# A windowed-attention block on one core: the key-value products moved in front of the convolution

## What is computed

```python
x = x + conv_bn(x, dw0_w, dw0_s, dw0_b, groups=C)       # depthwise 3x3
x = x + ffn(x, f0...)                                   # 1x1, relu, 1x1
x = x + windowed_attn(x, ...)                           # 7x7 windows, 4 heads of 16 channels
x = x + conv_bn(x, dw1_w, dw1_s, dw1_b, groups=C)
x = x + ffn(x, f1...)

# attention, in each window:
q, k, v = xw @ wq.T, xw @ wk.T + pos, xw @ wv.T
q, k = focus((relu(q) + 1e-6) / sc), focus((relu(k) + 1e-6) / sc)
#   focus(t) = t**3 / norm(t**3) * norm(t)
z   = 1 / (q @ k.sum(over tokens) + 1e-6)
y   = (q @ (k.T @ v)) * z + dwc(v)                      # dwc: depthwise 5x5 in the window
out = y @ proj_w.T + proj_b
```

## Time and profile before

| | |
|---|---|
| time, median of 3 runs | 210.66 us (209.52 to 211.52) |
| the profiled execution | 209.91 us |
| its span in the profile | 208.1 us, 4705 instructions |
| TensorE busy (matmul) | 184.5 us, 89% |
| VectorE busy | 127.4 us, 61% |
| ScalarE busy | 94.3 us, 45% |
| GpSimd busy | 34.6 us, 17% |
| mean granted TensorE clock | 0.984 of full speed |

### The profile page before, as it was taken

How to read it: one execution, slowest core, us unless ns; L and a number is a source line. 1 busy time by engine, 2 the same in 40 slices (tenths; PEclk the granted TensorE clock), 3 DMA queues, 4 the chain that set the end, 5 groups by cost and what they waited for, 6 DMA issues and landing times.

```text
span 208.1 us, 4705 instructions
## 1 busy us (share of the span) xinstructions
PE 184.5 (89%) x1938; PEld 98.4 (47%) x1938; DVE 127.4 (61%) x235; ACT 94.3 (45%) x152; POOL 34.6 (17%) x78
## 2 busy tenths in 40 slices
PE   7699963997997997999899979979979999899883
PEld 6224621352753753884464546528447844522210
DVE  3748496295599599419948975975994183122111
ACT  2462813238159159423832652581395315322431
POOL 1000350007007107000430160070052000000000
PEclk9999998599999999999999999999999999999999
DMA  6999917624000000000430161171044007666912
GB/s 141 216 250 214 204 38 156 173 73 72 3 0 5 0 3 0 0 6 0 142 72 2 57 159 54 45 165 54 0 120 144 3 20 183 161 171 163 255 56 95
DMA packets 15092, 19.12 MB, mean 92 GB/s; under 512 B 2160, under 2 KB 10608, under 8 KB 15072
## 3 DMA queue, kind: packets, MB, share of 16 engines
q1 hardware_dynamic: 13744, 17.63, 35.6%
q10 hardware_dynamic: 1328, 1.20, 2.3%
HBM read 14.50 MB, written 4.33 MB: 90 GB/s over the span
## 4 chain that ended last, share of the span: by engine, by line
PE 74%; ACT 9%; DVE 6%; issue 4%; DMA 4%; SPq 0%; POOL 0%; DVEq 0%; ACTq 0%; POOLq 0%
PE ps L471 15%; PE ps L495 9%; PE ps L606 8%; ACT kv L382 6%; PE ps L558 6%; PE ps L512 4%; PE ps L538 4%; PE ps L660 4%; PE ps L489 4%; PE ps L577 4%; PE ps L623 4%; PE ps L562 3%; DMA xr<-x_out 2%; PE ps L666 2%; PE ps L516 2%
## 5 line engine op out<-in xcount | busy, mean ns | idle before, releaser
L471 PE MATMUL ps<-xr,dwst 96*32 96x480 f32 (+1 forms) x384 | 43.3, 584 | 3.5 <-DVE x L751 1.8
L320 POOL TENSOR_SCALAR vmt<-vbot,cst 128x128 f32<-128x128 f32 x48 | 17.3, 385 | 122.4 <-PE ps L562 99.5
L495 PE MATMUL ps<-hid,w2t 128*64 128x512 f32 x64 | 23.3, 645 | 10.2 <-ACT hid L344 10.2
L344 ACT ACTIVATE hid<-ps,fst 128x512 f32<-128x512 f32 x32 | 20.2, 690 | 12.9 <-PE ps L489 12.9
L471 PEld LDWEIGHTS ps<-xr,dwst 96*32 96x32 f32 x384 | 11.2, 111 | 28.1 <-issue 25.3
L336 ACT ACTIVATE x<-ps,fst 128x512 f32<-128x512 f32 x16 | 10.9, 684 | 24.8 <-PE ps L471 24.8
L489 PE MATMUL ps<-x,w1t 64*128 64x512 f32 x64 | 18.1, 640 | 4.3 <-ACT x L336 3.3
L359 ACT ACTIVATE sq<-tqk 128x1280 f32<-128x1280 f32 x8 | 10.2, 1271 | 24.1 <-DVE tqk L779 23.4
L382 ACT ACTIVATE kv<-ps,cst 128x288 f32<-128x288 f32 x32 | 19.2, 765 | 3.0 <-PE ps L562 2.8
L606 PEld LDWEIGHTS ps<-qt,kv 64*64 64x64 f32 x576 | 17.4, 135 | 4.9 <-issue 4.8
L771 DVE TENSOR_TENSOR kraw<-ps,pose 128x640 f32<-128x640 f32 x8 | 6.6, 824 | 21.1 <-PE ps L516 21.1
(11 more groups left out here) (105 smaller groups left out, 256.0 us busy)
## 6 DMA issues: line engine op xcount, KB each, us to landing
xr<-x_out SPq DMA_DIRECT2D x16, 264.0 KB, 4.6
xr<-in_x SPq DMA_DIRECT2D x16, 240.0 KB, 6.3
x_out<-x SPq DMA_DIRECT2D x8, 272.0 KB, 2.5
xr<-x_out SPq DMA_DIRECT2D x8, 272.0 KB, 3.3
xr<-in_x SPq DMA_DIRECT2D x8, 256.0 KB, 5.2
out<-y SPq DMA_DIRECT2D x8, 256.0 KB, 2.3
tband<-in_matrix ACTq DMA_DIRECT2D x1, 784.0 KB, 5.1
wts<-in_weights SPq DMA_DIRECT2D x1, 416.0 KB, 8.4
```

What stands on the lines that cost most here:

```text
L320: last = eng.tensor_scalar(vmt[:, w, :, :], vbot[:, g, :, :], cc("win_bot")[:, w:w + 1], 0.0, ALU.mult, ALU.add)
L344: eng.activation(hid[:, m % 2, a, :], bank(P_H + a), ACT.Relu, bias=ff(f"f{s}b1")).then_inc(h_ready, 1)
L471: last = eng.matmul(dst[:, :, max(-dx, 0):HW - max(dx, 0)], dwst[:, s, tile % 2, dx + 1, :], taps_of(m, tile, dx), start=(dx == 0), stop=( ...
L495: last = eng.matmul(dw_bank(m)[64 * a:64 * a + 64], w2t[:, s, :], hid[:, m % 2, a, :], start=True, stop=True)
```

## The change

In the loop TensorE computes `key_value(g2)` directly behind `key_sum(g2)`, in front of the convolution instead of behind `project_v(g1)`. ScalarE's `take_kv(g2)` moves with it, in front of `widened`, and `take_v(g1)` goes behind `sixth(g1)`. In front of the loop the order of the first three groups is another one on TensorE, ScalarE and VectorE. No instruction is added or taken away, no wait is changed, and GpSimd's and SyncE's programs stay as they are.

```diff
@@ ScalarE @@
             squares(0)
             widened(2)
+            sixth(0)
+            hidden(2)
             take_v(0)
-            hidden(2)
-            sixth(0)
             ratio(0)
             widened(3)
...
                 squares(g1)
+                take_kv(g2)
                 widened(n + AHEAD)
+                sixth(g1)
                 take_v(g1)
-                sixth(g1)
-                take_kv(g2)
                 hidden(n + AHEAD)
@@ TensorE @@
             conv(2)
+            project_qk(1)
+            ffn1(2)
             project_v(0)
-            ffn1(2)
-            project_qk(1)
             ffn2(2)
...
                 key_sum(g2)
+                key_value(g2)
                 conv(n + AHEAD)
                 if 0 <= c:
                     project(c)
                 project_v(g1)
-                key_value(g2)
                 ffn1(n + AHEAD)
@@ VectorE @@
             cubes(0)
+            norm2(0)
             k_raw(1)
             q_t(1)
             k_t(1)
             residual(2)
-            norm2(0)
+            norm6(0)
             eng.wait_ge(pads_ps, 1)
             eng.tensor_tensor(projc[:, :], bank(7)[:, 447:448], ff("projb"), ALU.add).then_inc(projc_read, 1)
             eng.tensor_copy(kf[96:128, 0:8, :], bank(7)[96:128, 448:512].unsqueeze(1).broadcast_to([32, 8, C]))
             eng.tensor_copy(kf[0:32, 8:10, :], bank(7)[0:32, 448:512].unsqueeze(1).broadcast_to([32, 2, C])).then_inc(pads_taken, 1)
-            norm6(0)
```

## The result

| | before | after |
|---|---|---|
| time, median | 210.75 us (209.52 to 211.52, 4 runs) | 198.69 us (198.39 to 201.8, 4 runs) |
| ratio of the two, 95% interval | | 0.943 (0.937 to 0.949) |
| the profiled execution, its span | 209.91, 208.1 us | 198.42, 196.7 us |
| TensorE busy | 184.5 us, 89% | 182.4 us, 93% |
| mean granted TensorE clock | 0.984 | 1.000 |

The account below looks back on a forecast made before the run. TensorE's chain bound the kernel, with ScalarE's order making hid late and a slow start. 6.0 + 1.46 + 4.40 - 0.4 = 11.5 us took the profiled 209.91 to 198.4, median 198.8; range 196.5 to 203.0.

Parts of the forecast that it names:

- start and pass 2: From the program's start to pass 3: reordered first groups and pass 2 make pass 3 begin at 48.2, gaining 6.0 us.
- of it the clock: At the start: TensorE keeps full clock instead of falling to half, about 2.5 us of the 6.0 gained.
- passes 3 and 4: Main loop: hid starts earlier despite a new 0.5 us stall for q_t; 0.73 us each, 1.46 for two.
- passes 5 to 7: Main loop: hid no longer waits behind take_kv, so each pass takes 16.19 instead of 17.29 us, gaining 1.10.
- pass 8: Last loop pass: gains 1.10 us but loses 0.4 because the window convolution's bank comes free late.
- rival (2): At the start the clock falls all the same: 2.5 us less gain, 201.3 us, chance 0.12.
- Passes 5 to 8: Main loop: no stall for q_t, turn_q hidden before ffn2's second half; 1.10 us a pass, 4.40 for four.
- VectorE's round: VectorE's work per loop pass: 15.9 to 16.0 us against TensorE's 16.19, hidden by 0.2 to 0.3.
- the 200.0 us: Loop: q_final and k_focus meeting GpSimd's masks cost 0.27 us each, VectorE binds at 16.5; 1.2 us in all.
- The rival of the masks (7): Slower kernel: GpSimd's masks, their slack cut from 10.8 to 3.9 us, delay key_value; some 213 us, chance 0.02.
- The tail: After pass 8: keeps its order and only moves, with no gain or loss counted.
- The cover for the transfers: Loop: transfers stay covered, as attended moves 1.7 us later and the conv reading its result 2.1 later.

Follow-up runs that it names:

- the queries first: Changed kernel with q_scale and q_final moved in front of attended on VectorE in the loop; 199.5 us, ratio 0.949.
- a third of the masks: Changed kernel with only three of nine GpSimd masks made for groups 1 to 7; 200.57 us.
- the old copies: Changed kernel with ScalarE's loop order as before the change, TensorE and the start as changed; 234.86 us, ratio 1.129.
- fillers behind it: Kernel before with eight extra matmuls, results unread, between conv(3) and ffn1(3) on TensorE; 210.38 us.

## Right or wrong, step by step

The prediction was right, and nearly term by term (us gained; the measured ones are from the two profiled executions):

| step | predicted | measured |
|---|---|---|
| start and pass 2 | 6.0 | 6.2 |
| of it the clock | 2.5 | 2.54 |
| passes 3 and 4 | 1.46 | 1.31 |
| passes 5 to 7 | 3.30 | 3.11 |
| pass 8 | 1.10 - 0.4 = 0.7 | 0.68 |
| sum | 11.5 | 11.3 |

That the median (198.69) came within 0.1 us of 198.8 is in part luck: the terms are off by 0.2, 0.15 and 0.19 with different signs, and the tail's wait for a transfer was 0.5 us in both profiled executions, though it is 1.4 us or more in eleven of the twelve other runs.

**The start.** `residual(2)` was put at 27.2 and came at 27.09, `conv(3)` at 28.1 (27.98), `x1(3)` at 30.85 (30.72), `ffn2(3)`'s end at 35.1 (35.01), pass 3 at 48.2 (48.03). Its parts are now separate: 2.63 from the order up to `ffn1(3)` (17.48 to 14.85 behind the first projection), 2.54 from the clock, 1.04 from the loop's order in pass 2. The judgement that the clock would stay up held: TensorE's waits were 0.26, 0.80 and 0.77 us (forecast 0.7, 0.8 and 0.8), so rival (2) did not come. The old order of VectorE, with 2.46 us in front of `ffn1(3)`, brings the fall back.

**Passes 3 and 4.** `key_value` waits 0.5 for `q_t`, as worked out, and ScalarE is tight behind it: `sixth`, `vband` and `vbot` are in the chain there. The gain is 0.15 smaller because each pass takes 0.1 more than the 15.15 and 20.04 that the terms gave: `key_value` starts 3.43 into the pass, not 3.33. `hid` starts at 10.65, where the prediction wrote 10.57 and its own terms add up to 10.50 to 10.55. And the last link is not `hid` alone: `turn_q`, which needs the copied values, is ready last by the chain, a link that the prediction doesn't have there.

**Passes 5 to 8.** The wait for `hid` is gone and no wait for `q_t` came. One word was wrong: `turn_q` was called hidden. It is the last to be ready, is over at 12.80 of the pass, and the whole of `ffn2` still follows it, up to 14.04; by way of `hid`, as the run with the queries first shows, it is 14.05. So two chains bind the pass, which the prediction did not see. The 0.05 us between 16.19 and 16.24 are not this: `key_value` takes 2.17 us (103.05 to 105.22), where the terms had 2.12. In pass 8 the loss is where it was forecast, at the window convolution's bank: 0.38 us over 16.24 + 4.89, against 0.4, and 0.35 of it goes away with the queries first.

**VectorE's round** was given 0.2 to 0.3 us of slack, and it has 0.1 (wait of 0.26 with a third of the masks, less the 0.16 that `k_focus` is shorter there) to 0.2 (band masks twice). The meeting with the masks is real but costs 0.16 us, not 0.54, and so the 200.0 us did not come: `q_final` takes 0.76 and 0.28 us as before, and only the first 0.3 us of `k_focus` lie beside a mask in pass 6. The Trainium skill, page "GPSIMD Engine Reference", section "1. Specifications", has the two engines contend for the shared interfaces when VectorE reads two SBUF inputs; `k_focus` does, and the traces agree (in pass 6: 1.29 us without masks beside it, 1.45 as changed, 2.24 and 5.34 beside more of them).

**The rival of the masks (7)** was put aside for a sound reason, nothing in the kernel makes masks of 8 us, but its deciding point was incomplete. The wait of `key_value` that it names does come when the masks last 9.4 us (43.4 to 52.8), in passes 3 and 4; the slack there is 3.1 us (masks end at 48.4, `key_value` starts at 51.5), not the 3.9 of pass 6. In the passes behind, `k_focus` gives way first: VectorE has almost no slack, so that band masks made twice cost time already, without any wait on a mask.

**The tail** only moved, as said. The cover for the transfers was enough in the profiled execution, and is the least sure part of the kernel. The wait for the input of `conv(15)` was 0.5 us, but 1.4 with the queries first and 1.5 with a third of the masks, whose passes are the same. The chains of the changed kernel and of the one with the queries first show the transfer ahead of it:

```profile
176.96 3.17 DMA x_out<-x
```

```profile
176.69 4.07 DMA x_out<-x
```

Why the same transfer takes 3.2 us in one and 4.1 in another wasn't tried. It is about as large as the spread of one kernel's runs, and the median of the changed kernel would carry it too.

## What to carry to other kernels

When an engine waits early in a pass and is late at its end, reorder it against the moment at which each input appears: here a copy of 2.2 us and a square of 1.2 us went into two holes of ScalarE, and 5.1 us came out of passes 3 to 8. Follow the new order round every engine and write down the slacks: those under 0.3 us are the first to look at for the next bound, and two chains that are level must be shortened together. Read the granted clock behind each wait of TensorE, since a wait can cost more than its length: 2.5 us more at this start, 1.3 us more in pass 6 of the kernel with the old copies, 2.8 with all masks twice.

## What was not expected of the hardware

- The clock fell to 0.50 already behind one wait of 1.8 us in front of `conv(3)` in the kernel with fillers behind it, while in the kernel before it fell only behind the second wait, near 35. Between otherwise equal starts the moment of the fall differs by up to 5 us, and what decides it stays open.
- One VectorE instruction with two SBUF inputs, of 281 ns, took 4.28 us while six of GpSimd's masks followed each other, until they were over; with the band masks alone made twice the same instruction took 681 ns, got through before their end, and the masks slowed as well (2.03 to 2.53 us for three); in pass 3 of the changed kernel itself it took 680. What decides between the two is open; it wasn't tried.
